# A second attention layer on one core: projection and other fills issued between a slot's scores and its transposes, ranking scores first

## The reference

```python
qkv = x @ W_attn.T + b_attn                    # x: 4 x 512 x 128; 16 heads of 64
att = q @ k.T / sqrt(64), causal
S   = relu(att[head 0]), column 0 and the diagonal zeroed
FF  = cumsum of S over the queries, shifted by one
att = att - FF                                 # every head
keep, for each query, the int(0.2 * 512) keys with the smallest FF, and the diagonal
y   = softmax(att where kept) @ v
y   = y @ W_proj.T + b_proj
```

## Time and profile before

| what | value |
| --- | --- |
| median of 3 runs | 1010.16 us (1009.35 to 1012.23) |
| span of the profiled execution | 1014.7 us (the page gives no other time of it) |
| busy: PE, DVE, ACT, POOL | 89%, 72%, 63%, 53% |
| granted clock of PE, mean | 0.946 |
| second attention in the profile | about 467 to 890 us |

### The profile page before, as it was taken

One profiled execution on the slowest core, in us unless ns is written; L12 is line 12 of the kernel. 1 busy time (PEld: TensorE's weight loads), 2 busy tenths in 40 slices (PEclk: granted clock), 3 DMA queues, 4 the chain that ended last, 5 costly groups with the idle time before them and its releaser, 6 DMA issues. The chain is left out here.

```text
span 1014.7 us, 19335 instructions
## 1 busy us (share of the span) xinstructions
PE 905.4 (89%) x6140; PEld 606.1 (60%) x6140; DVE 734.6 (72%) x2087; ACT 643.8 (63%) x1433; POOL 537.6 (53%) x664
## 2 busy tenths in 40 slices
PE   8899989998999999988999999989998988962396
PEld 5444444444678888865556666656665755652296
DVE  5676777763889999877997978697878878444022
ACT  2566656554778888844867677767777767740174
POOL 4234536243703344001668766877777778942344
PEclk9999999986999999999999999999999989985599
DMA  4000001000444433140000000000000000002882
GB/s 137 1 1 1 22 1 44 1 24 10 121 138 127 131 104 111 35 120 1 2 1 2 1 2 1 2 1 2 2 1 2 1 2 1 2 1 67 278 286 95
DMA packets 31130, 47.73 MB, mean 47 GB/s; under 512 B 3804, under 2 KB 18673, under 8 KB 30912
## 3 DMA queue, kind: packets, MB, share of 16 engines
q1 hardware_dynamic: 29104, 43.42, 14.2%
q0 software_dynamic: 1504, 3.17, 0.9%
q10 hardware_dynamic: 432, 0.01, 0.0%
HBM read 40.25 MB, written 6.79 MB: 46 GB/s over the span
## 5 line engine op out<-in xcount | busy, mean ns | idle before, releaser
L1507 POOL TENSOR_SCALAR probs<-probs,rinv 128x128 f32<-128x128 f32 (+3 forms) x256 | 274.7, 1086 | 102.1 <-DVE rinv L1372 102.0
L1442 ACT ACTIVATE probs<-probs,rowmin 128x128 f32<-128x128 f32 (+3 forms) x256 | 141.7, 559 | 30.1 <-DVE rowmin L1366 29.0
L1366 DVE CUSTOM_DVE_ANT_0 probs<-psum,adj 128x128 f32<-128x128 f32 (+3 forms) x256 | 122.2, 478 | 50.0 <-PE psum L1227 49.4
L1451 ACT ACTIVATE pt<-psum 128x128 f32<-128x128 f32 (+3 forms) x256 | 98.4, 435 | 69.1 <-PE psum L1237 66.9
L841 ACT ACTIVATE pT<-psum 128x1024 f32<-128x1024 f32 (+3 forms) x128 | 89.6, 702 | 61.9 <-PE psum L597 60.9
L1227 PE MATMUL psum<-k_sb,q_sb 64*128 64x256 f32 (+3 forms) x512 | 110.5, 484 | 17.5 <-DVE rowmin L1366 17.2
L769 DVE TENSOR_REDUCE top<-psum 128x2 f32<-128x256 f32 (+3 forms) x128 | 102.3, 818 | 19.7 <-PE psum L577 19.5
L1355 DVE MAX8 top<-w 128x8 f32<-128x131 f32 (+3 forms) x208 | 103.1, 496 | 4.6
L1815 ACT ACTIVATE r_hid<-psum,b1t 128x512 f32<-128x512 f32 x125 | 82.8, 689 | 33.0 <-PE psum L1654 28.8
L1237 PEld LDWEIGHTS psum<-ident,probs 128*128 128x128 f32 x640 | 68.4, 142 | 58.3 <-POOL probs L1507 37.6
L1237 PE MATMUL psum<-ident,probs 128*128 128x128 f32 x640 | 99.5, 286 | 0.8 <-POOL probs L1507 0.8
(11 more groups left out here) (306 smaller groups left out, 1914.1 us busy)
## 6 DMA issues: line engine op xcount, KB each, us to landing
r_share<-shares SPq DMA_DIRECT2D x12, 1024.0 KB, 7.1
s_wb<-in_w_all SPq DMA_DIRECT2D x23, 514.5 KB
sorted_x<-blank SPq DMA_DIRECT2D x1, 2967.0 KB, 11.9
s_xg<-sorted_x SPq DMA_DIRECT2D x23, 129.0 KB, 2.8
r_w1s<-in_w SPq DMA_DIRECT2D x16, 128.0 KB, 5.8
r_w2s<-in_w SPq DMA_DIRECT2D x16, 128.0 KB, 6.2
r_share<-shares SPq DMA_DIRECT2D x6, 256.0 KB, 3.4
r_share<-shares SPq DMA_DIRECT2D x2, 768.0 KB, 5.0
```

Of the source, the lines that this page charges most:

```text
L1366: dve.tensor_tensor_reduce(probs[:, k, 0:K], s_bank[h][:, 0:K], adj[:, OFF[i]:OFF[i] + K], 1.0, FLOOR, ALU.add, ALU.min, rowmin[:, k:k + 1 ...
L1442: act.activation(probs[:, k, 0:K], probs[:, k, 0:K], ACT.Exp, bias=rowmin[:, k:k + 1], scale=-1.0, accum_out=rsum[:, k:k + 1]).then_inc(ex ...
L1451: act.activation(pt[:, (2 * n + h) % 4, 0:K], t_bank[h][:, 0:K], ACT.Copy).then_inc(pt_ready, 1)
L1507: pool.tensor_scalar(probs[:, k, 0:K], probs[:, k, 0:K], rinv[:, k:k + 1], None, ALU.mult).then_inc(normed, 1)
```

## The change

In each step PE issued the scores of step n, the transposes of step n - 3, the product with v of step n - 4 and then the fills of step n. Now the fills stand directly behind the scores. And where a step of a next batch has an `rs`, it stands first of the step's fills, ahead of `out`, `q` and `k`; this also decides which bank each fill has and which fill it waits for.

```diff
                 if b + 1 < B:
+                    if l in RS_AT:
+                        out.insert(0, ("rs", b + 1, RS_AT.index(l)))
                     if l == X_AT:
                         out.append(("x", b + 1, 0))
...
-                    if l in RS_AT:
-                        out.append(("rs", b + 1, RS_AT.index(l)))
...
                     for n in range(NSTEP):
                         if n < NS:
                             pe_score(pe, n)
+                        for use in fills_at(n):
+                            pe_fill(pe, use)
                         if TURN_LAG <= n < NS + TURN_LAG:
                             pe_turn(pe, n - TURN_LAG)
                         if PV_LAG <= n < NS + PV_LAG:
                             pe_pv(pe, n - PV_LAG)
-                        for use in fills_at(n):
-                            pe_fill(pe, use)
```

## The result

The changed kernel takes 1031.93 us (median of four runs, 1028.92 to 1037.46). The ratio of its runs to those of the kernel before is 1.0207, with a 95% interval of 1.0160 to 1.0254. It is slower, by some 21 us: the kernel before, run beside it, has a median of 1011.08 us (four runs). The interval, 16 to 26 us, leaves open whether that is more or less than 2%. The forecast was 1036, in a range of 1013 to 1046.

What follows compares the result with a forecast made beforehand. PE was taken to bound the stage. New waits of 30.2 us for ACT's drains, less 1.2 and 2.5 given back, made +26.5, scaled to 26.4; from 1010.2 that gave 1036 us, own range 1025 to 1042, 8 in 10 range 1013 to 1046.

Steps and rivals of the forecast that it cites:

- The chain: From the product with v through ACT's copies, exponentials and drain to PE's next fill: 2.2 us at K = 256.
- (b): Fills' first matmul, now behind scores and ahead of transposes, costs as much or 0.1 less: 2.5 us saved in 85 steps.
- rival 3: Faster: PE changes array shape three times per fill step, not four; 9.4 us come back, 1000 without new waits; 10%.
- (a): Ranking scores (rs), now behind the scores, may overlap the second head's last part: 1.2 us saved over 12.
- (c): DVE gets rs and `out` sooner: worth nothing as PE is the bound; late score waits (l = 26 to 29) stay.
- Rival 1: Partly absorbed: drains come earlier at K = 384, those waits vanish and the K = 256 part halves: 1019; 16%.
- rival 2: DVE falls behind too: PE waits for the second bias at l = 8, 12, 16, 20: +7, 1043; 10%.

Runs made afterwards that it cites:

- experiment 3: Changed kernel, but ACT takes out the fills of step n in its round n, ahead of the copies: 1021.3 us, ratio 1.0082.
- experiment 4: Changed kernel, but ACT does the exponentials of step n ahead of the copies of step n - 3, drains still a round late: 1024.37 us, ratio 1.0110.
- experiment 6: Changed kernel, but with the fills between the transposes and the product with v: 1009.34 us, ratio 0.9973.
- experiment 10: Kernel before (fills last on PE), but ACT takes out the fills of step n in round n, ahead of the copies: 1046.04 us, ratio 1.0343.
- experiment 2: Kernel before with only the rs lines of the diff, so rs is the first fill of its step: 1016.35 us, ratio 1.0032.
- experiment 7: Kernel before, with fills ahead of the transposes only in chosen steps (l = 29 to 31, 0 to 4, 17, 22): 1008.74 us, ratio 0.9975.
- experiment 9: Kernel before, fills between transposes and v except l = 7, 8, 12 to 15; ACT drains in the same round at n = 0 to 2: 1001.84 us, ratio 0.9902.
- Experiment 5: The kernel of experiment 3, with DVE also taking rs out in the round of its own step: 1014.2 us, ratio 1.0008.

## Why the prediction was right, and where its sizes were off

The mechanism of the waits was the predicted one, and experiments 3, 4, 6 and 10 show it from four sides: give ACT the new order, shorten its chain, move the fill back behind the transposes, or put ACT alone in the new order. Of what the change gives back, one term was too small and one had the wrong sign. The waits, for the second batch where nothing else is said:

| place | forecast | measured wait |
| --- | --- | --- |
| q at l = 8, behind x | 1.6 | 1.47 |
| k at l = 10 | 0.65 | 0.27 |
| q at l = 11 | 1.1 | 0.97 |
| k at l = 12 | 1.1 | 0.86 |
| `out` at l = 13 | 1.2 | 0.92 |
| k at l = 14; q at l = 15 | 0.45; 0.15 | 0.22; 0 |
| q, k, `out` at l = 19 to 21 | 1.0, 1.1, 1.4 | 0.86, 0.96, 1.23 |
| v, v, v, x of the first batch, n = 4 to 7 | 1.1, 1.0, 1.0, 1.0 | 1.34, 0.88, 0.88, 0.88 |

- *The whole sum.* Over the four batches PE's waits rose by (10.9 + 8.1 + 8.1 + 1.3 =) 28.4 us, for which I had 30.2. PE's busy time fell by (0.3 + 2.6 + 2.6 + 1.5 =) 7.0, for which I had 3.7. So the net is 21.4 by these figures, where the sum had 26.5 (which gives 1036.6, not 1036), and of the 5 us too much some 2 lie in the waits and 3 in what the change gives back. The last batch came out as forecast (-0.1), but by two terms that I had near nothing: 1.3 us more waits for DVE and 1.5 us less work.
- The chain was 0.1 to 0.4 us too long at nearly every place, and too short at the first v. At l = 11 it was 2.04, where I had 2.2. PE's added waits came to 8.1 us in the batch, where the forecast had 9.5.
- The first batch's waits rose by 10.9 us (18.5 against 7.6); the forecast, with DVE's waits taken off, was 11.2. That is luck: two errors cancel. The waits of fills at l = 10 to 21 came to 6.5 us, where I had 8.3, and 1.8 of them are for DVE (rs at l = 13, 1.03; `dec` at l = 19, 0.79), for whose fills I had said 0. The scores' waits for DVE, on the other hand, did not disappear. They are 4.3 us now against 4.8; at l = 18 and 19 they are 0.58 and 0.89, where I had them gone. And of the 10.7 us by which this batch grew, 1.6 come from a fall of the clock at n = 1.
- What the change gives back was sized too low: (3.7 / 3 =) 1.2 us a batch against 2.6 measured as PE's lost busy time. The term that was off is (b), the cheaper neighbours, for which I took 0.03 us a step from a range of 0 to 0.11; 2.6 us in 26 steps are 0.10. With rival 3's price for it, 9.4 us, the sum gives 1029.7; the measured 1031.9 lies between the two forecasts. Where nothing waits a fill step became 0.15 us shorter (l = 30: 4.00 to 3.85). Its start and end in the kernel before:

```profile
574.40 1.13 PE L1227 MATMUL psum<-k_sb,q_sb 64*128 64x512 f32 x4
578.40 1.13 PE L1227 MATMUL psum<-k_sb,q_sb 64*128 64x512 f32 x4
```

The timeline after:

```profile
582.29 1.13 PE L1227 MATMUL psum<-k_sb,q_sb 64*128 64x512 f32 x4
583.35 0.50 PE L1188 MATMUL psum<-wv_hi,xb_hi 128*128 128x512 f32 x1
583.69 0.39 PE L1189 MATMUL psum<-wv_lo,xb_hi 128*128 128x512 f32 x1
583.92 0.39 PE L1190 MATMUL psum<-wv_hi,xb_lo 128*128 128x512 f32 x1
584.15 1.03 PE L1237 MATMUL psum<-ident,probs 128*128 128x128 f32 x8
585.12 1.09 PE L1253 MATMUL psum<-pt,v_sb 128*64 128x128 f32 x16
586.14 1.13 PE L1227 MATMUL psum<-k_sb,q_sb 64*128 64x512 f32 x4
```

From the fill's last matmul to the transposes are 0.23 us, the pace inside a fill; from a fill to scores it was 0.33. Another 0.06 us goes from the transposes' own time (1.03 to 0.97). The rule of the Trainium skill ("TensorEngine Tiling (Array Packing)", Key Properties) that a change of tiling mode drains the array fits this: transposes and fills share a mode. The number format is not the reason: the fills' inputs are fp32r, those of transposes, scores, rs and `dec` are fp32. In the kernel before a fill is followed after 0.31 us by rs (616.87 to 617.18), which has 64 rows like the scores, but after 0.23 by `dec` (637.60 to 637.83), which has the fills' 128 x 128. The slow first matmul of a fill, from which rival 3 took its 0.11, is another thing: it takes 0.34 us to the next behind the product with v and still 0.31 behind `out` (621.02 to 621.33), which has the fills' own shape. So at most 0.03 of that lies in the shape, and rival 3 had nearly the right size from the wrong place.
- (a) had the wrong sign. I gave rs 1.2 us for overlapping the scores behind which it now stands, and missed that it overlapped the next scores before (experiment 2). At l = 15 rs adds 0.93 us to PE's way now (636.76 to 638.32, less 0.63 for the scores), where it added 0.85 before (628.02 to 630.03, less the 1.16 that the same way took without one, 631.78 to 632.94). An estimate from this place is that (a) costs some 0.1 us for each of the 12.
- (c): no gain from DVE's earlier rs and `out` is to be seen, and the late score waits stayed (0.91, 0.85, 0.95 in the second batch).
- Rival 1, partly absorbed, is out: at K = 384 the waits are 0.86, 0.96 and 1.23. So is rival 2, DVE behind as well: in the second batch the scores of l = 8, 12, 16 and 20 don't wait for DVE, and the two new score waits, at l = 1 and 7, are 0.17 and 0.23 us.
- Rival 3, faster, had its saving right in kind and fell on its condition. Experiments 7 and 9 are that rival with the waits kept away; in 9 the gain is clear of the noise, in 7 at its edge.

## What to carry to other kernels

Where a producer's queue and a consumer's queue are both written out by hand, moving one item in one of them moves everything behind the matching item in the other. Before such a move, walk the loop from the item through the consumer's queue, in its order, back to the buffer that the next item needs, and set it against the work that the producer has in between; a few durations of the old trace gave every wait in the table within 0.4 us. And try the other gaps: here the place between transposes and product with v had cheaper neighbours without the wait, and gave the largest gain, 1%. Look in the old trace, too, for what already overlaps at the item's old place: moving it gives that up.

## What was not expected of the hardware

The clock fell in the first batch of some kernels and not of others, with waits of much the same length. In the kernel with ACT's drains in the same round, PE had stood idle for 1.78 us (the q behind x, l = 8), and its matmuls then began 0.43 us apart where they had been 0.23; the granted clock of 490 to 500 us was 0.66. Experiment 5 has the same wait of 1.78 and fell too, for less long (0.83). The changed kernel had waited there for 1.48 us and kept 1.00, but fell at n = 1, behind two waits of 1.1 and 0.7 us that the kernel before has too, without a fall. Its six L1205 matmuls there took 2.77 us against 1.46. That fall cost 1.6 us, the one in experiment 3 about 6, by PE's busy time. So a wait of one or two us on PE was followed by a fall in some executions and not in others, and a difference of a few us between single executions can be that. What decides between them is open here.
